# A fused attention kernel on one core: part 0's sums in its own steps, and the side jobs of each image in other steps

## The chip, the core and the metric

The kernel runs on one core of a Trainium2 chip. The metric is device time in microseconds (us) of that core, lower is better. The engines that matter are TensorE (PE: matmuls, with its weight loads PEld), VectorE (DVE), ScalarE (ACT), GpSimd (POOL), and the queue of SyncE (SP), which issues most transfers.

## The reference, cut to what matters

```python
def _L0_conv_ref(x, Wq, bq, Wk, bk, Wv, bv, gamma):      # x: (8, 128, 32, 32)
    xf = x.reshape(b, c, n)                              # n = 1024 pixels
    q = jnp.einsum('oc,bcn->bon', Wq, xf) + bq[None, :, None]      # 64 channels
    k = jnp.einsum('oc,bcn->bon', Wk, xf) + bk[None, :, None]
    v = jnp.einsum('oc,bcn->bon', Wv, xf) + bv[None, :, None]      # 128 channels
    attn = jax.nn.softmax(jnp.einsum('bci,bcj->bij', q, k), axis=-1)
    out = jnp.einsum('bcn,bmn->bcm', v, attn).reshape(b, c, h, w)
    return gamma * out + x
```

Eight images, each a self-attention over its 1024 pixels, all in fp32.

## The kernel before, in words

**Steps and parts.** Each image is cut into 16 steps (`STEPS`), 128 steps in all. A part is four steps (`PART_STEPS`) and 256 queries (`PART`): an image has four parts, and a step of a part takes two tiles of 128 keys. Two parts make a chunk of 512 queries. All five engines walk the same step numbers `s = 16*b + k` in a program written out by hand; semaphores tie them together. Nothing is scheduled by a planner: the order in the source is the order on each engine.

**Accuracy.** Values are split into a rounded high part and the rest. The scores of a step are two matmuls for each key tile (high and low halves of q and k stacked on the partitions, and the row of maxima as an extra row). ACT reads them twice (`exponentials`): once exact into `weight`, once rounded into `weight_hi`. The rest, `weight_lo`, is a subtraction (`low_weights`): on POOL for three steps of a part, and on DVE in the third (`low_on_dve`), where ACT writes the exact weights into a PSUM bank of the part's own sums instead (`exact_weights`, bank `sums[:, 1]` for even parts and `sums[:, 3]` for odd ones).

**PE's steps.** In step s PE makes the scores of step s+2 (`score_tile`, `AHEAD` = 2), one to three row maxima matmuls for later queries (`do_max`), the high sums of step s-2 (`sums_hi`, `LAG` = 2), at the end of a part the sixteen low sums (`sums_lo`), and the side jobs of the step: "qk" projects q and k of the image after next, half an image at a time; "v" projects V of the next image, by halves; "mt" turns maxima into a row (image 0 only; later images send them by DMA in `send_max_row`). In image 0 the maxima of images 0 and 1 have to be caught up with (`EARLY_MAXES`, 18 steps; an entry is chunk, first index, count).

**The two work banks.** Every maximum and every side job writes one of two PSUM banks, in turn (`WORK_ORDER`, `bank_of`). A job waits in `take_bank` until the job two places before it has been read out: a maximum by one DVE reduction (`maximum`); "qk" by ACT (`round_qk`) and then DVE (`rest_of_qk`); "v" by ACT (`round_v`) and then DVE (`rest_of_v`).

**The side chains.** ACT rounds x (`round_x`), POOL makes its rest (`rest_of_x`), PE projects, ACT and DVE round. Then SP spreads q and k over the partitions by DMA (`spread`; `spread_by_halves` for image 1, whose q and k and whose second half of image 0's V are projected straight into sums banks before and in steps 1 and 2). `round_qk` for the first half of an image waits until the spread of the image before has landed, since that spread reads the same tile. POOL makes the short copy of V (`short_values`) and adds the bias to x (`add_bias`). After a part's low sums ACT takes half of them (`take_low_sum`), DVE inverts and adds (`invert`, `add_low`), and `finish` writes y in the step `finish_step(part)`: six steps after the part's first, but eight for part 0. A sums bank is free when y of its part is done (`y_done`).

In step s, ACT does `exponentials(s + 2)`, then the rounding jobs; DVE the side jobs of step s-1, the maxima of s, `low_weights(s + 1)` if it is its turn, then `invert`, `add_low` and `finish`; POOL `low_weights(s + 1)` if it is its turn, then its side work.

Of the kernel before, what the change touches and what calls it, by code (L numbers as in the profile page):

```python
# [26 lines left out]
LAG = 2  # L27
# [21 lines left out]
               7: (2, 0, 2), 8: (2, 2, 2), 9: (2, 4, 1), 10: (2, 5, 1), 11: (2, 6, 2),  # L49
               12: (3, 0, 2), 13: (3, 2, 1), 14: (3, 3, 1), 15: (3, 4, 2), 16: (3, 6, 1), 17: (3, 7, 1)}  # L50

MAX_TURNS = {0: ("mt", 0, 1), 3: ("mt", 1, 0), 7: ("mt", 1, 1)}
# [11 lines left out]
def side_jobs(s):  # L64

    b, k = divmod(s, STEPS)
    jobs = []
    if s in MAX_TURNS:
        jobs.append(MAX_TURNS[s])
    if k in (6, 10) and b + 2 < BATCHES:  # L70
        jobs.append(("qk", b + 2, (6, 10).index(k)))
    if k in (11, 15) and b + 1 < BATCHES:
        jobs.append(("v", b + 1, (11, 15).index(k)))
    return jobs
# [17 lines left out]
def low_on_dve(s):  # L92
    return s % PART_STEPS == DVE_LOW
# [15 lines left out]
def finish_step(part):  # L109
    return PART_STEPS * part + PART_STEPS + AHEAD + (2 if part == 0 else 0)  # L110
# [29 lines left out]
def attention_program(nc, x, x_turned, Wq, bq, Wk, bk, Wv, bv, gamma, out):  # L140
# [9 lines left out]
    with ExitStack() as ctx:  # L150
# [275 lines left out]
        def _(pool):  # L426
# [67 lines left out]
            for s in range(ALL_STEPS):  # L494
# [5 lines left out]
                if k in (0, 12) and s > 0 and b + k // 12 < BATCHES:  # L500
                    short_values(b + k // 12, 1 - k // 12)
                if s in (4, 8):
                    add_bias((4, 8).index(s))
                if b == 0 and k in (5, 9) or b > 0 and k in (1, 5) and b + 2 < BATCHES:
                    rest_of_x(b + 2, (5, 9).index(k) if b == 0 else (1, 5).index(k))
                if b == 0 and k in (10, 13) or b > 0 and k in (9, 13) and b + 1 < BATCHES:
                    add_bias(2 * (b + 1) + k // 13)

        @block.tensor
        def _(pe):  # L510
# [87 lines left out]
            def sums_hi(s):  # L598
# [9 lines left out]
                if j == 0:  # L608

                    wait(pe, y_done, PAIR * (u - 1))  # L610
                    pe.wait_ge(weight_lo_done, low_count(s + DVE_LOW))
# [73 lines left out]
            pe.wait_ge(neg_max_done, CHUNK_TILES + 1)  # L685
            project_v(0, 1, sums[:, 0])
# [4 lines left out]
            for s in range(ALL_STEPS + LAG):  # L691
# [5 lines left out]
                if LAG <= s < ALL_STEPS:  # L697
                    if s == LAG:

                        pe.wait_ge(first_v_rest_done, 1)  # L700
                        pe.wait_ge(neg_max_done, CHUNK_TILES + PAIR)
                    if s == LAG + PART_STEPS:

                        pe.wait_ge(qk_lo_done, HALVES)
                    sums_hi(s - LAG)
                    if (s - LAG) % PART_STEPS == PART_STEPS - 1:
                        sums_lo(s - LAG)
                if s in (1, 2):
# [321 lines left out]
```

## Time and profile before

| | |
|---|---|
| time, median of 3 runs | 240.18 us (240.05 to 241.45) |
| time of the profiled execution | 239.82 us |
| its span in the profile | 238.0 us |
| PE busy | 221.8 us (93%) |
| ACT, POOL, DVE busy | 177.9, 177.5, 161.0 us (75%, 75%, 68%) |

The profiled execution's span covers all but 1.8 us of its own time. A busy time counts instructions of an engine; the matmuls of PE overlap in its pipeline, so that its pace is read from the starts of successive instructions rather than from their durations. All times of the trace are in us from the start of the span.

### The profile page before, as it was taken

Reading aid. Unit: us, or ns where it says so; the run is one execution under the profiler, and the core shown is the slowest. Engines: PE = TensorE matmul, PEld = TensorE weight load, DVE = VectorE, ACT = ScalarE, POOL = GpSimd, SP = SyncE. Lnnn points to the kernel's source line nnn. Section 1 sums busy time; section 2 is a strip of 40 time slices with the busy share of each in tenths; the row PEclk is TensorE's granted clock in tenths of the full one; section 3 lists DMA queues with packets and bytes.
Section 4 is the critical chain, followed back from the end, with each engine's and each line's share of the span. In section 5 each row is a group of like instructions: output and inputs, shape, how many; then the busy total and the mean of one; then the engine's idle time right before and its main releaser. Section 6 shows DMA issues by size and latency. Waiting matters only on the chain.

```text
span 238.0 us, 5352 instructions
## 1 busy us (share of the span) xinstructions
PE 221.8 (93%) x1864; PEld 205.0 (86%) x1864; DVE 161.0 (68%) x345; ACT 177.9 (75%) x342; POOL 177.5 (75%) x162
## 2 busy tenths in 40 slices
PE   6786958799999999999999999999999999999994
PEld 5464857599998999899998999899998999999994
DVE  1676556787776677777776677767776687676334
ACT  2486856668887798778877798778877788778980
POOL 8667665967877788778887787778886866886871
PEclk9999999999999999999999999999999999999999
DMA  3652640067700945048600964039400862100111
GB/s 95 212 211 64 156 136 1 4 144 166 223 0 3 234 120 178 2 106 208 214 10 0 218 153 164 2 89 221 139 0 0 196 159 88 49 0 3 44 48 44
DMA packets 17882, 24.43 MB, mean 103 GB/s; under 512 B 9920, under 2 KB 10688, under 8 KB 17856
## 3 DMA queue, kind: packets, MB, share of 16 engines
q1 hardware_dynamic: 17552, 23.96, 38.6%
q8 instruction: 15, 0.25, 0.5%
q10 hardware_dynamic: 304, 0.13, 0.2%
q14 instruction: 11, 0.09, 0.1%
HBM read 8.59 MB, written 4.19 MB: 54 GB/s over the span
## 4 chain that ended last, share of the span: by engine, by line
PE 80%; DVE 6%; ACT 4%; DMA 3%; issue 3%; POOL 2%; SPq 1%; ACTq 0%; POOLq 0%
PE sums L615 22%; PE sums L629 12%; PE scores L594 11%; PE scores L595 11%; PE work L550 10%; PE work L544 6%; ACT qk_hi L746 2%; DVE qk_lo L840 2%; DMA k_hione<-qk_hi 2%; DMA w_qk<-in_L_conv_Wk 1%; PE work L537 1%; PE work L539 1%; PE work L538 1%; PE sums L550 1%; DVE neg_max L849 1%
## 5 line engine op out<-in xcount | busy, mean ns | idle before, releaser
L476 POOL TENSOR_TENSOR weight_lo<-weight,weight_hi 128x512 bf16<-128x512 f32 x96 | 123.1, 1290 | 40.7 <-ACT weight_hi L788 40.6
L849 DVE TENSOR_REDUCE neg_max<-work 128x1 f32<-128x512 f32 x120 | 82.0, 686 | 12.2 <-PE work L550 12.2
L615 PEld LDWEIGHTS sums<-values,weight_hi 128*128 128x128 f32 x504 | 76.6, 189 | 6.7 <-issue 2.0
L615 PE MATMUL sums<-values,weight_hi 128*128 128x258 f32 x504 | 80.8, 282 | 1.7 <-DVE weight_lo L887 1.7
L788 ACT ACTIVATE weight_hi<-scores 128x512 fp32r<-128x512 f32 x128 | 76.4, 597 | 0.0
L594 PE MATMUL scores<-q_hihi,k_hilo 128*128 128x256 f32 x256 | 71.0, 300 | 0.5 <-ACT weight_hi L788 0.5
L595 PE MATMUL scores<-q_lomax,k_hione 128*128 128x256 f32 x256 | 66.2, 281 | 0.0
L785 ACT ACTIVATE weight<-scores 128x512 f32<-128x512 f32 x96 | 57.5, 599 | 10.0 <-PE scores L595 3.6
L550 PE MATMUL work<-k_hilo,q_hihi 128*128 128x512 f32 x120 | 48.4, 406 | 4.7 <-DVE qk_lo L840 3.3
L594 PEld LDWEIGHTS scores<-q_hihi,k_hilo 128*128 128x128 f32 x256 | 48.3, 189 | 2.1 <-issue 1.6
L595 PEld LDWEIGHTS scores<-q_lomax,k_hione 128*128 128x128 f32 x256 | 48.5, 189 | 1.0 <-issue 0.5
L629 PE MATMUL sums<-values_b,weight_lo 128*128 128x130 bf16 x496 | 34.4, 221 | 0.0
L629 PEld LDWEIGHTS sums<-values_b,weight_lo 128*128 128x128 bf16 x496 | 28.9, 98 | 1.4
L550 PEld LDWEIGHTS work<-k_hilo,q_hihi 128*128 128x128 f32 x120 | 22.6, 188 | 6.6 <-issue 2.7
L887 DVE TENSOR_TENSOR weight_lo<-sums,weight_hi 128x512 bf16<-128x512 f32 x32 | 22.0, 686 | 6.6 <-ACT weight_hi L788 6.6
L794 ACT ACTIVATE low_sum<-sums 128x256 f32<-128x256 f32 x31 | 11.9, 385 | 13.3 <-PE sums L629 13.3
L845 DVE TENSOR_TENSOR values<-work,values 128x512 fp32r<-128x512 f32 x14 | 9.7, 692 | 18.0 <-ACT values L757 18.0
L457 POOL TENSOR_TENSOR x_lo<-x_sb,x_hi 128x512 fp32r<-128x512 f32 x12 | 15.3, 1277 | 8.4 <-ACT x_hi L753 8.4
L785 ACT ACTIVATE sums<-scores 128x512 f32<-128x512 f32 x32 | 19.0, 592 | 3.0 <-DVE y_sb L912 2.3
L484 POOL TENSOR_TENSOR x_turned_sb<-x_turned_sb,gamma_bv 128x512 f32<-128x512 f32 x16 | 20.6, 1285 | 0.0
L912 DVE SCALAR_TENSOR_TENSOR y_sb<-sums,one_over,x_turned_sb 128x128 f32<-128x128 f32 x62 | 18.7, 343 | 0.7 <-DVE sums L892 0.4
L544 PE MATMUL work<-w_v_t,x_sb 128*128 128x128 f32 x112 | 15.4, 280 | 2.0 <-DVE qk_lo L840 1.9
(85 smaller groups left out, 162.4 us busy)
## 6 DMA issues: line engine op xcount, KB each, us to landing
x_turned_sb<-in_x_turned SPq DMA_DIRECT2D x8, 512.0 KB, 4.6
out<-y_sb SPq DMA_DIRECT2D x15, 256.0 KB, 3.4
x_sb<-in_x SPq DMA_DIRECT2D x7, 512.0 KB, 4.5
q_hihi<-qk_hi SPq DMA_DIRECT2D x12, 256.0 KB, 4.4
q_lomax<-qk_lo SPq DMA_DIRECT2D x7, 256.0 KB, 5.7
k_hione<-qk_hi SPq DMA_DIRECT2D x7, 256.0 KB, 5.2
k_hilo<-qk_hi SPq DMA_DIRECT2D x6, 256.0 KB, 3.2
k_hilo<-qk_lo SPq DMA_DIRECT2D x6, 256.0 KB, 5.1
```

The lines of the kernel that those rows point to most:

```text
L476: pool.tensor_tensor(weight_lo[:, r], weight[:, r], weight_hi[:, r], ALU.subtract).then_inc(weight_lo_pool_done, 1)
L484: pool.tensor_tensor(place, place, bias, ALU.add).then_inc(with_bias_done, 1)
L544: last = pe.matmul(place[:, tile(t)], image(n)[:, tile(half * CHUNK_TILES + t)], w_v_t[:, :], start=True, stop=True)
L550: pe.matmul(place, q_hihi[p][:, tile(t)], k_hilo[p][:, chunk(h)], start=True, stop=True).then_inc(mx_done, 1)
L594: pe.matmul(place, k_hilo[p][:, keys], q_hihi[p][:, queries], start=True, stop=False)
L595: last = pe.matmul(place, k_hione[p][:, keys], q_lomax[p][:, queries], start=False, stop=True)
L615: last = pe.matmul(sums[:, u % 2 * PAIR + it, 0:VCOLS], weight_hi[:, r, part_tile(kt, it)], values[p][:, key_tile(s, kt)], start=(j == 0 a ...
L629: last = pe.matmul(sums[:, u % 2 * PAIR + it, CHANNELS:VCOLS], weight_lo[:, i % RING, part_tile(kt, it)], values_b[p][:, key_tile(i, kt)], ...
L785: act.activation(exact_weights(s) if low_on_dve(s) else weight[:, r], scores[:, s % 2], ACT.Exp)
L788: act.activation(weight_hi[:, r], scores[:, s % 2], ACT.Exp).then_inc(weight_hi_done, 1)
L849: dve.reduce_max(neg_max[:, t, h:h + 1], place, AX.X, negate=True).then_inc(neg_max_done, 1)
L887: dve.tensor_tensor(weight_lo[:, r], exact_weights(s), weight_hi[:, r], ALU.subtract).then_inc(weight_lo_done, 1)
```

## The change: what it does

- Part 0 (steps 0 to 3): `sums_hi(s)` runs in step s itself and not in step s+2. All four low weights of this part are made on POOL (`low_on_dve` starts with part 1), so that its sums banks are not lent out, and `sums_hi` of part 0 no longer waits for them. The second half of image 0's V goes to bank `sums[:, 2]` (waiting for one more pair of first maxima), q and k of image 1 to banks 3 and 2. DVE takes the first maximum of chunk 1 ahead of the rest of V. The low sums of part 0 stay in step 5.
- y of part 0 is finished in step 6, not 8.
- Side jobs: q and k of the image after next in steps 7 and 11 (before 6 and 10), and in steps 10 and 13 of image 0; V of the next image in steps 3 and 15 (before 11 and 15), and in 7 and 15 of image 0. x is rounded in steps 4 and 8, and its rest made in 5 and 9, in every image (before, 0 and 4, 1 and 5 behind image 0). The short copies of V and the biases follow the new places.
- The early maxima are dealt out a little differently over steps 7 to 17, and two turns of maxima stand one step later (4 and 8).

```diff
--- before.py
+++ after.py
@@ -46,10 +46,13 @@
 
 EARLY = 18
 EARLY_MAXES = {0: (1, 1, 1), 1: (1, 2, 1), 2: (1, 3, 1), 3: (1, 4, 1), 4: (1, 5, 1), 5: (1, 6, 1), 6: (1, 7, 1),
-               7: (2, 0, 2), 8: (2, 2, 2), 9: (2, 4, 1), 10: (2, 5, 1), 11: (2, 6, 2),
-               12: (3, 0, 2), 13: (3, 2, 1), 14: (3, 3, 1), 15: (3, 4, 2), 16: (3, 6, 1), 17: (3, 7, 1)}
-
-MAX_TURNS = {0: ("mt", 0, 1), 3: ("mt", 1, 0), 7: ("mt", 1, 1)}
+               7: (2, 0, 1), 8: (2, 1, 2), 9: (2, 3, 2), 10: (2, 5, 1), 11: (2, 6, 2),
+               12: (3, 0, 1), 13: (3, 1, 1), 14: (3, 2, 2), 15: (3, 4, 1), 16: (3, 5, 2), 17: (3, 7, 1)}
+
+MAX_TURNS = {0: ("mt", 0, 1), 4: ("mt", 1, 0), 8: ("mt", 1, 1)}
+QK_STEPS, FIRST_QK_STEPS = (7, 11), (10, 13)
+V_STEPS, FIRST_V_STEPS = (3, 15), (7, 15)
+X_HI_STEPS, X_LO_STEPS = (4, 8), (5, 9)
 
 
 def max_jobs(s):
@@ -67,10 +70,11 @@
     jobs = []
     if s in MAX_TURNS:
         jobs.append(MAX_TURNS[s])
-    if k in (6, 10) and b + 2 < BATCHES:
-        jobs.append(("qk", b + 2, (6, 10).index(k)))
-    if k in (11, 15) and b + 1 < BATCHES:
-        jobs.append(("v", b + 1, (11, 15).index(k)))
+    qk_steps, v_steps = (FIRST_QK_STEPS, FIRST_V_STEPS) if b == 0 else (QK_STEPS, V_STEPS)
+    if k in qk_steps and b + 2 < BATCHES:
+        jobs.append(("qk", b + 2, qk_steps.index(k)))
+    if k in v_steps and b + 1 < BATCHES:
+        jobs.append(("v", b + 1, v_steps.index(k)))
     return jobs
 
 
@@ -90,7 +94,7 @@
 
 
 def low_on_dve(s):
-    return s % PART_STEPS == DVE_LOW
+    return s >= PART_STEPS and s % PART_STEPS == DVE_LOW
 
 
 def low_count(s):
@@ -107,7 +111,7 @@
 
 
 def finish_step(part):
-    return PART_STEPS * part + PART_STEPS + AHEAD + (2 if part == 0 else 0)
+    return PART_STEPS * part + PART_STEPS + AHEAD
 
 
 def max_count(chunk, i):
@@ -497,14 +501,18 @@
                     low_weights(s + 1)
                 if s == 0:
                     short_values(0, 1)
-                if k in (0, 12) and s > 0 and b + k // 12 < BATCHES:
-                    short_values(b + k // 12, 1 - k // 12)
-                if s in (4, 8):
-                    add_bias((4, 8).index(s))
-                if b == 0 and k in (5, 9) or b > 0 and k in (1, 5) and b + 2 < BATCHES:
-                    rest_of_x(b + 2, (5, 9).index(k) if b == 0 else (1, 5).index(k))
-                if b == 0 and k in (10, 13) or b > 0 and k in (9, 13) and b + 1 < BATCHES:
-                    add_bias(2 * (b + 1) + k // 13)
+                if k == 0 and b > 0:
+                    short_values(b, 1)
+                if k == (10 if b == 0 else 6) and b + 1 < BATCHES:
+                    short_values(b + 1, 0)
+                if s == 4:
+                    add_bias(0)
+                if k == (8 if b == 0 else 1):
+                    add_bias(HALVES * b + 1)
+                if k in X_LO_STEPS and b + 2 < BATCHES:
+                    rest_of_x(b + 2, X_LO_STEPS.index(k))
+                if k == 13 and b + 1 < BATCHES:
+                    add_bias(HALVES * (b + 1))
 
         @block.tensor
         def _(pe):
@@ -608,7 +616,8 @@
                 if j == 0:
 
                     wait(pe, y_done, PAIR * (u - 1))
-                    pe.wait_ge(weight_lo_done, low_count(s + DVE_LOW))
+                    if u > 0:
+                        pe.wait_ge(weight_lo_done, low_count(s + DVE_LOW))
                 pe.wait_ge(weight_hi_done, s + 1)
                 for kt in range(PAIR):
                     for it in range(PAIR):
@@ -682,8 +691,8 @@
             for s in range(AHEAD):
                 score_tile(s)
 
-            pe.wait_ge(neg_max_done, CHUNK_TILES + 1)
-            project_v(0, 1, sums[:, 0])
+            pe.wait_ge(neg_max_done, CHUNK_TILES + PAIR + 1)
+            project_v(0, 1, sums[:, PAIR])
             pe.wait_ge(first_hi_done, len(FIRST))
             for name, c, i in FIRST_MAXES:
                 do_max(c, i)
@@ -694,20 +703,24 @@
                 if s < ALL_STEPS:
                     for c, i in max_jobs(s):
                         do_max(c, i)
-                if LAG <= s < ALL_STEPS:
-                    if s == LAG:
-
-                        pe.wait_ge(first_v_rest_done, 1)
+                if s < PART_STEPS:
+                    if s == 0:
+
                         pe.wait_ge(neg_max_done, CHUNK_TILES + PAIR)
-                    if s == LAG + PART_STEPS:
+                    sums_hi(s)
+                elif PART_STEPS + LAG <= s < ALL_STEPS:
+                    if s == PART_STEPS + LAG:
 
                         pe.wait_ge(qk_lo_done, HALVES)
                     sums_hi(s - LAG)
-                    if (s - LAG) % PART_STEPS == PART_STEPS - 1:
-                        sums_lo(s - LAG)
-                if s in (1, 2):
-                    pe.wait_ge(neg_max_done, CHUNK_TILES + PAIR + s)
-                    project_qk(1, s - 1, sums[:, PAIR + s - 1])
+                if LAG <= s < ALL_STEPS and (s - LAG) % PART_STEPS == PART_STEPS - 1:
+                    sums_lo(s - LAG)
+                if s == 1:
+                    pe.wait_ge(neg_max_done, MAXES)
+                    project_qk(1, 0, sums[:, PAIR + 1])
+                if s == 2:
+                    pe.wait_ge(first_v_rest_done, 1)
+                    project_qk(1, 1, sums[:, PAIR])
                 if s < ALL_STEPS:
                     for job in side_jobs(s):
                         do_job(job)
@@ -778,8 +791,6 @@
                 if low_on_dve(s):
                     u = s // PART_STEPS
                     wait(act, y_done, PAIR * (u - 1))
-                    if u == 0:
-                        act.wait_ge(neg_max_done, CHUNK_TILES + PAIR)
                     if u == 1:
                         act.wait_ge(qk_lo_done, HALVES)
                 act.activation(exact_weights(s) if low_on_dve(s) else weight[:, r], scores[:, s % 2], ACT.Exp)
@@ -815,7 +826,7 @@
             write_max_rows(1, 0, 0, PART, scores[:, 1])
             exponentials(0)
             first_q(1, bank(0))
-            round_v(0, 1, sums[:, 0])
+            round_v(0, 1, sums[:, PAIR])
             exponentials(1)
 
             for s in range(ALL_STEPS):
@@ -823,13 +834,13 @@
                 if s + AHEAD < ALL_STEPS:
                     exponentials(s + AHEAD)
                 if s in (1, 2):
-                    round_qk(1, s - 1, sums[:, PAIR + s - 1])
+                    round_qk(1, s - 1, sums[:, PAIR + 2 - s])
                 if s >= LAG and (s - LAG) % PART_STEPS == PART_STEPS - 1:
                     take_low_sum((s - LAG) // PART_STEPS)
                 for job in side_jobs(s):
                     do_job(job)
-                if b == 0 and k in (4, 8) or b > 0 and k in (0, 4) and b + 2 < BATCHES:
-                    round_x(b + 2, (4, 8).index(k) if b == 0 else (0, 4).index(k))
+                if k in X_HI_STEPS and b + 2 < BATCHES:
+                    round_x(b + 2, X_HI_STEPS.index(k))
 
             store_last(act, 1)
 
@@ -952,11 +963,11 @@
             dve.wait_ge(first_hi_done, len(FIRST))
             dve.scalar_tensor_tensor(q_lomax[0][0:HEAD, chunk(1)], bank(0)[0:HEAD, :], b_qq[0:HEAD, :],
                                      q_hihi[0][0:HEAD, chunk(1)], ALU.add, ALU.subtract).then_inc(first_q_rest_done, 1)
-            dve.wait_ge(v_hi_done, HALVES)
-            dve.tensor_tensor(values[0][:, quarter(1), 0:CHANNELS], by_tiles(sums[:, 0]),
-                              values[0][:, quarter(1), CHANNELS:2 * CHANNELS], ALU.subtract).then_inc(first_v_rest_done, 1)
             for name, c, i in FIRST_MAXES:
                 do_max(c, i)
+            dve.wait_ge(v_hi_done, HALVES)
+            dve.tensor_tensor(values[0][:, quarter(1), 0:CHANNELS], by_tiles(sums[:, PAIR]),
+                              values[0][:, quarter(1), CHANNELS:2 * CHANNELS], ALU.subtract).then_inc(first_v_rest_done, 1)
 
             for s in range(ALL_STEPS):
                 b, k = divmod(s, STEPS)
@@ -966,7 +977,7 @@
                 for c, i in max_jobs(s):
                     do_max(c, i)
                 if s in (1, 2):
-                    rest_of_qk(1, s - 1, sums[:, PAIR + s - 1])
+                    rest_of_qk(1, s - 1, sums[:, PAIR + 2 - s])
                 if s + 1 < ALL_STEPS and low_on_dve(s + 1):
                     low_weights(s + 1)
                 if s >= LAG and (s - LAG) % PART_STEPS == PART_STEPS - 1:
```

## Rows read from the trace of the kernel before

**Rows 1.** The page: PE's busy time, and the chain that ended last by engine.

```profile
PE 221.8 (93%) x1864; PEld 205.0 (86%) x1864; DVE 161.0 (68%) x345; ACT 177.9 (75%) x342; POOL 177.5 (75%) x162
...
PE 80%; DVE 6%; ACT 4%; DMA 3%; issue 3%; POOL 2%; SPq 1%; ACTq 0%; POOLq 0%
```

**Rows 2.** Busy time over one image: length, then PE, PEld, DVE, ACT, POOL, clock.

```profile
71.80:98.80 27.00, 26.61 (x232) 25.15 (x232) 19.81 (x43) 21.91 (x42) 21.54 (x19) 1.00 0.46 118
```

**Rows 3.** Waits on PE: us in total, times, longest.

```profile
PE work L544 <- DVE qk_lo L840: 1.9, 5, 0.4
```

**Rows 4.** Timeline of PE, image 2: start, duration, instruction, idle before.

```profile
100.35 1.16 PE L544 MATMUL work<-w_v_t,x_sb 128*128 128x128 f32 x8 [0.39 <-DVE qk_lo L840]
...
102.53 0.28 PE L594 MATMUL scores<-q_hihi,k_hilo 128*128 128x256 f32 x1
...
103.00 0.42 PE L550 MATMUL work<-k_hilo,q_hihi 128*128 128x512 f32 x1
...
103.26 0.65 PE L615 MATMUL sums<-values,weight_hi 128*128 128x258 f32 x4
...
120.76 0.50 PE L550 MATMUL work<-k_hilo,q_hihi 128*128 128x512 f32 x1
```

**Rows 5.** The chain in order of time: start, us on the chain, what.

```profile
19.21 0.87 PE sums L533 x2
...
102.21 0.49 PE sums L615 x4
...
103.91 0.95 PE sums L629 x16
...
107.29 0.89 PE work L544 x8
```

**Rows 6.** Timeline of the start, steps up to the first part's end.

```profile
12.31 2.47 DVE L849 TENSOR_REDUCE neg_max<-sums 128x1 f32<-128x512 f32 x4
...
18.12 0.28 PE L555 MATMUL work<-identity_r,neg_max_r 128*1 128x128 f32 x2 [0.70 <-DVE neg_max L849]
...
20.83 0.75 DVE L840 SCALAR_TENSOR_TENSOR qk_lo<-sums,b_qk,qk_hi 128x512 fp32r<-128x512 f32 x1 [0.89 <-ACT qk_hi L746]
...
22.44 0.72 PE L615 MATMUL sums<-values,weight_hi 128*128 128x258 f32 x4 [1.66 <-DVE weight_lo L887]
...
29.09 0.37 PE L594 MATMUL scores<-q_hihi,k_hilo 128*128 128x256 f32 x1
```

**Rows 7.** Timeline of steps 7 to 18.

```profile
32.72 0.69 ACT L746 ACTIVATE qk_hi<-work,b_qk 128x512 fp32r<-128x512 f32 x1 [1.78 <-DMA k_hione<-qk_hi]
...
34.34 0.47 PE L550 MATMUL work<-k_hilo,q_hihi 128*128 128x512 f32 x1 [2.41 <-DVE qk_lo L840]
...
38.14 0.58 ACT L785 ACTIVATE sums<-scores 128x512 f32<-128x512 f32 x1 [2.33 <-DVE y_sb L912]
...
41.36 0.47 PE L537 MATMUL work<-x_hi,w_qk_hi 128*128 128x512 f32 x1 [0.46 <-POOL x_lo L457]
...
43.87 0.50 PE L550 MATMUL work<-k_hilo,q_hihi 128*128 128x512 f32 x1 [0.87 <-DVE qk_lo L840]
...
45.32 2.58 SPq L378 DMA_DIRECT2D q_lomax<-neg_max_r  x4
...
57.31 0.36 PE L594 MATMUL scores<-q_hihi,k_hilo 128*128 128x256 f32 x1
```

**Rows 8.** The page's groups: busy, mean ns of one, then idle before.

```profile
L476 POOL TENSOR_TENSOR weight_lo<-weight,weight_hi 128x512 bf16<-128x512 f32 x96 | 123.1, 1290 | 40.7 <-ACT weight_hi L788 40.6
```

**Rows 9.** Issue to landing of the maxima rows (L378), steps 11 to 19.

```profile
DMA to landing us min/median/max: 1.9/2.0/2.1
```

**Rows 10.** The spread and its reader one image on: SP and PE, timeline.

```profile
78.09 1.16 SPq L353 DMA_DIRECT2D k_hilo<-qk_lo  x1
...
84.85 0.40 PE L550 MATMUL work<-k_hilo,q_hihi 128*128 128x512 f32 x1
```

**Rows 11.** Issue to landing of the last spread that maxima need (L353).

```profile
DMA to landing us min/median/max: 4.9/5.1/6.3
```

## The prediction

> **What bounds the kernel now.** I read the busy times and the chain first, then PE's waits, then the start step by step. PE is busy for 93% of the span and the last chain lies on it for 80% [rows 1]. Behind the start an image takes 27.0 us, of which PE is busy for 26.6 and ACT, POOL and DVE for about 20 to 22 [rows 2]. So the bound is PE's stream of matmuls, none of which the change adds or removes: the time can move only by PE's stalls. Where they are: five times 0.4 us before a V job [rows 3], and many in the first 57 us, where step 18 starts at 57.31 [rows 7]. What a step costs PE when it never waits comes from one undisturbed step: scores 0.47 (102.53 to 103.00), a maximum 0.25 (103.00 to 103.26; 0.24 where nothing holds it) [rows 4], high sums 0.48, low sums 0.95, half a V 0.89, half of image 1's q and k 0.87 [rows 5]; half a q and k of a later image is three 512-column matmuls at the pace of the maximum, 0.7. ACT's two exponentials take about 0.6 each, from the one at 38.14 [rows 7]; with their overlap I use 1.2 a pair. Four DVE maxima take 2.47 [rows 6], so 0.62 one, 0.67 with a hand-off; a POOL subtraction 1.29 [rows 8].
>
> **Part 0's sums in its own steps.** Before, PE waits 0.70 for a work bank ahead of the first turn [rows 6] and 1.66 in step 2, where the high sums need the low weights of step 2, which DVE makes only behind `rest_of_qk` (20.83 to 21.58, itself idle for 0.89 behind ACT) [rows 6]. After, I walk the steps. The V half in bank 2 needs seven first maxima; four run from 12.31 to 14.78 [rows 6], so the seventh is read at about 14.2, before PE asks at 14.7: no cost. Step 0: scores from 16.5, maximum, high sums, done at 17.7; DVE has by then read the first maximum (0.67 sooner, as the rest of V now follows it), and the turn waits for nothing. Step 1: scores to 18.3, but the maximum's bank is read only behind the rest of V and one maximum, at 18.9: **a new stall of 0.6**. High sums and q and k end at 20.5. Step 2 ends at 22.6, step 3 (no side job) at 23.8. Step 4 has no sums; its turn waits for a maximum that DVE makes behind the second `rest_of_qk`, until 25.0 (0.5 of stall). Step 5 ends with the low sums at 26.9. Before, step 6 begins at 29.09 [rows 6]. **Gain so far 2.2.**
>
> The price of the move is one subtraction more on POOL. POOL makes low weights 0 to 3 by 22.1 in my walk and PE wants them at 25.9, so 1.29 is hidden with 3.8 to spare. It frees DVE by about a maximum's time before its second q and k. On the 1.29: POOL's subtractions average 1290 ns over 96 cases, beside a DVE that is busy two thirds of the time [rows 1, 8], so I see no stretching. The Trainium skill, "SBUF — State Buffer", section "SBUF: two separate sides", says the pair of ports that DVE and GpSimd share is an exclusive lock, taken on DVE's side by two-port modes or by two SBUF inputs. DVE's two-input instructions here have one input in PSUM, so by the rule as by the row nothing is added; if the lock did bite, each POOL subtraction could wait for a whole DVE instruction, 0.7 more, and the 3.8 us of cover would be eaten to about 1.
>
> **Steps 6 to 9: q and k of image 2 later, V of image 1 sooner.** Before, ACT's rounding of the q and k of step 6 waits until the spread of image 1 has landed (1.78 idle, start at 32.72), and PE waits 2.41 for the bank [rows 7]. After, q and k stand in step 10, which PE reaches at 35.5; the spread is issued about 1 us sooner than before and lands at about 31.7. That stall goes whole. What is late next: V in step 7 waits 0.4 for the maximum of step 6, which DVE makes behind `invert` and `add_low`; the maxima of step 8 wait for V's two roundings and one maximum, 0.8 in all. Step 10 starts at 35.5. Before, PE was through with step 9 at about 38.9: from 34.34 on the rest of step 7 is 0.8, step 8 with two maxima 1.45, step 9 with its low sums 2.15, and some 0.1 of refilling. **Gain 3.4 to 3.5** (2.2, plus 2.4, less 1.2, and V's 0.9 for q and k's 0.7 in these steps).
>
> **y of part 0 sooner.** Before, `exponentials(10)` writes into part 0's bank and waits 2.33 for y, until 38.14; PE then stalls for 0.5 before the scores of step 10 [rows 7]. After, y is done at 30.6 (low sum taken at 28.5, bias added on POOL at 27.3), while ACT asks at 31.5. That stall goes, and so does the 0.5 before 41.36 where the rest of x had waited behind that same ACT delay [rows 7]. **Gain 4.6 at the start of step 11** (37.5 against 42.1, which is 41.36 and q and k's 0.7).
>
> **Steps 11 to 18.** Removed: 0.9 at 43.87 behind q and k [rows 7] and about 0.9 behind V. New: the same kind behind the q and k of step 10 (0.9), one of 0.65 behind the V of step 15, and one of another kind: the row of image 1's maxima. Before, it is sent as soon as it is rounded, in four issues from 45.32 taking 2.58 [rows 7], and the last, issued 1.9 later, lands in 2.0 [rows 9], so 4.0 behind the rounding. The stretch in question (from the last maximum to the first scores of image 1) then holds a V and its wait more. After, the rounding is at 40.65, the row lands at 44.7, and PE, with fewer stalls between, asks at 43.9: **0.8 of new stall**. V and q and k change places at 0.1 to 0.2. Step 18 starts at about 52.65 against 57.31: still **4.65**. The spread of image 2 is now issued behind the q and k of step 13, from about 44.9; its last needed transfer is issued 1.9 later and lands in 4.9 to 6.3 [rows 11], so at 51.7 to 53.0. The maximum that reads it comes at 53.2. No cost, but with 0.2 to 1.5 to spare.
>
> **The later images.** Before, V directly follows q and k and waits for their bank: 0.39 of idle, and about 0.16 more (an estimate: the matmul ahead is still draining for 0.16, its 0.64 less the pace of 0.48) [rows 4], five times [rows 3]. After, it is a maximum two places behind the q and k of step 11, as it is already behind those of step 6: there it costs 0.2 (120.76, pushed back by 0.1, and its longer 0.50) [rows 4]. So 0.35 by five images is **1.75**. Between nothing (the hand-off only moves) and 2.75 (five holes of 0.55) the row of the same kind decides. V in step 3 stands in a part as V in step 15 does, which costs nothing. POOL's and ACT's moved jobs have the same lengths and POOL is idle for a fifth of an image [rows 2]. SP's order is unchanged: its spread waits for the scores of step 15 in any case, which by my count come 0.5 behind the rounding of the q and k of step 11.
>
> **The sum.** 4.65 + 1.75 = 6.4 off the profiled 239.82, so 233.4; the median was 0.36 above the profiled execution, so **233.8**. The start is between 2.2 (only its first term holds) and about 9 (none of my new stalls appears); I take 3.2 to 6.5 as its reasonable ends.
>
> **The rivals.**
> - **Hand-offs come back (0.22).** My walk finds seven small new stalls where DVE or ACT must read a bank; ACT with 1.2 of exponentials a step is barely slower than PE in the start. If each is 0.3 to 0.5 longer than I have, or the spread of image 2 is late, the start gives 2 to 3.5 and the images 1: 235.5 to 237. For it: the row of maxima and the spread both have under 1.5 to spare. Against: before, such waits of PE lie under 1 us each save two.
> - **More than the sum (0.10).** DVE gets ahead and the stalls in steps 1, 8 and 14 vanish: about 2.5 more, 231 to 232.
> - **Slower (0.05).** The spread of every image. Before, its last needed transfer (issued at 78.09 for the maximum at 84.85) has 0.5 to 1.9 to spare [rows 10, 11]. If q and k a step later (1.2 us, or 2.1 where a part ends) became what SP waits for, instead of the scores of step 15, PE would stand before the first maximum of images 2 to 7. It loses once the rounding is more than 0.5 behind those scores; beyond 1.1 a time for six images it eats the whole gain, 240 to 244. Against: my count has the rounding ahead of the scores.
> - **It does not do what it says (0.05).** If low weights or V still come last in part 0 and POOL is behind from step 4 on, the early gain is given back at the first y, and 238 to 240 stays.
> - My forecast, 232 to 235.5, has 0.58.
>
> The range 231.5 to 237.0 leaves out the slow ends and the fast tail of the second rival. A measurement of this kernel can tell about 1%, 2.4 us; within that are the cases above 237.8: same 0.07, slower by more 0.03, faster 0.90.
>
> **What would show it.** In the profile after: the high sums of step 0 near 17.2; step 6's scores near 26.9; ACT's first q and k of image 2 without a DMA wait; `exponentials(10)` without a wait for y; PE's first scores of image 1 at about 44.7, perhaps with a wait for the row; step 18 near 52.7; an image of 26.6 to 26.7 instead of 27.0, with no V job waiting for q and k. It would be wrong if image 1's maxima row or image 2's spread holds PE for more than 1 us, or if an image takes 27.0 or more.

## The result, and the profile after

The changed kernel takes 233.26 us (median of 4 runs, 232.98 to 233.76) against 240.12 us (median of 4): a ratio of 0.9707 with a 95% interval of 0.9666 to 0.9749. The prediction said 233.8, range 231.5 to 237.0. The profiled execution took 233.76 us, with a span of 232.0.

The page of the changed kernel, busy times and chain, which answer to [rows 1]:

```profile
PE 221.5 (96%) x1864; PEld 205.0 (88%) x1864; DVE 159.7 (69%) x344; ACT 178.1 (77%) x342; POOL 178.0 (77%) x163
...
PE 85%; DVE 6%; DMA 4%; ACT 2%; SPq 1%; issue 1%; ACTq 0%
```

PE's busy time is what it was, to 0.3 us, as it must be with the same 1864 matmuls; the span lost its stalls. DVE has one instruction less and POOL one more: the low weights of step 2.

Where the time went can be read by laying the two timelines of PE against each other at the start of each step (the first score matmul of the tile made in that step):

| step | before, us | after, us | difference |
|---|---|---|---|
| 0 | 16.48 | 16.72 | +0.24 |
| 6 | 29.09 | 26.86 | -2.23 |
| 10 | 39.48 | 35.11 | -4.37 |
| 11 | 42.14 | 37.08 | -5.06 |
| 14 | 50.07 | 44.70 | -5.37 |
| 18 | 57.31 | 52.80 | -4.51 |
| 34 | 84.29 | 79.31 | -4.98 |
| 66 | 138.32 | 132.41 | -5.91 |
| 98 | 192.34 | 185.51 | -6.83 |
| 117 | 220.17 | 213.35 | -6.82 |
| 118 | 222.06 | 215.98 | -6.08 |
| 125 | 229.87 | 223.80 | -6.07 |

Counted from step 0, the start gives 4.75 us by step 18. Then five images give 0.42 to 0.50 each, 2.32 in all. Then something takes 0.74 back in one step, 117 to 118. PE's waits in the changed kernel (us in total, times, longest):

```profile
PE work L558 <- DVE values L856: 1.4, 2, 0.7
PE scores L602 <- DMA q_lomax<-neg_max_r: 1.4, 2, 0.9
PE work L558 <- DVE qk_lo L851: 0.9, 1, 0.9
```

The start, as the timeline of the changed kernel shows it (start, duration, instruction, idle before and its releaser):

```profile
17.50 0.65 PE L624 MATMUL sums<-values,weight_hi 128*128 128x258 f32 x4
18.00 0.28 PE L563 MATMUL work<-identity_r,neg_max_r 128*1 128x128 f32 x2
18.96 0.50 PE L558 MATMUL work<-k_hilo,q_hihi 128*128 128x512 f32 x1 [0.15 <-DVE neg_max L860]
...
25.00 0.28 PE L563 MATMUL work<-identity_r,neg_max_r 128*1 128x128 f32 x2 [0.26 <-DVE neg_max L860]
...
25.94 1.11 PE L638 MATMUL sums<-values_b,weight_lo 128*128 128x130 bf16 x16
26.86 0.36 PE L602 MATMUL scores<-q_hihi,k_hilo 128*128 128x256 f32 x1
...
27.81 0.61 ACT L796 ACTIVATE weight<-scores 128x512 f32<-128x512 f32 x1
28.80 0.60 ACT L796 ACTIVATE weight<-scores 128x512 f32<-128x512 f32 x1
...
30.89 0.59 ACT L796 ACTIVATE sums<-scores 128x512 f32<-128x512 f32 x1
31.78 0.50 PE L558 MATMUL work<-k_hilo,q_hihi 128*128 128x512 f32 x1 [0.71 <-DVE values L856]
...
38.81 0.50 PE L558 MATMUL work<-k_hilo,q_hihi 128*128 128x512 f32 x1 [0.86 <-DVE qk_lo L851]
...
40.26 2.44 SPq L382 DMA_DIRECT2D q_lomax<-neg_max_r  x4
...
44.70 0.38 PE L602 MATMUL scores<-q_hihi,k_hilo 128*128 128x256 f32 x1 [0.85 <-DMA q_lomax<-neg_max_r]
...
49.89 0.50 PE L558 MATMUL work<-k_hilo,q_hihi 128*128 128x512 f32 x1 [0.71 <-DVE values L856]
...
52.80 0.36 PE L602 MATMUL scores<-q_hihi,k_hilo 128*128 128x256 f32 x1
```

The high sums of step 0 stand at 17.50, where the kernel before had its first at 22.44 [rows 6]. The turn follows without a wait. ACT's exponentials of step 10, which had idled 2.33 us for y [rows 7], start at 30.89 with no idle in front; ACT's first q and k of image 2 has no DMA wait either. What is left are three bank hand-offs of 0.7 to 0.9 us behind a V or a q and k, and a wait of 0.85 us for the row of maxima. A wait costs more than its listed idle, since idle is counted from the end of the last matmul in the pipeline and not from the time when the next could have started. The maximum at 37.56 takes 0.24 of PE's pace, so the next could start at 37.80; it starts at 38.81, a hole of 1.0 for 0.86 of idle. "With the refill" below means such a hole.

A later image in the changed kernel, by stretch from step 34 to step 50 (columns as in [rows 2]), and the V job and the maximum behind q and k that answer to [rows 4]:

```profile
79.31:105.91 26.60, 26.60 (x235) 25.21 (x232) 19.68 (x43) 21.92 (x42) 21.40 (x19) 1.00 0.46 120
```

```profile
97.50 0.50 PE L558 MATMUL work<-k_hilo,q_hihi 128*128 128x512 f32 x1
...
101.69 1.05 PE L552 MATMUL work<-w_v_t,x_sb 128*128 128x128 f32 x8
```

PE's busy time now fills the stretch: 26.60 of 26.60. The V job waits for nothing. The maximum of step 13 has a duration of 0.50 in place of 0.39: a small late start, without idle, is all that the q and k of step 11 cost.

### The profile page after: what moved, and what is told of

The parts are those of the page before. It is cut to its first block, busy times and chain, and to the rows that moved or that the text cites. A ratio compares the mean times of both kernels' runs of the same rounds, so it can differ in the third digit from the quotient of the medians.

```text
span 232.0 us, 5350 instructions
## 1 busy us (share of the span) xinstructions
PE 221.5 (96%) x1864; PEld 205.0 (88%) x1864; DVE 159.7 (69%) x344; ACT 178.1 (77%) x342; POOL 178.0 (77%) x163
## 4 chain that ended last, share of the span: by engine, by line
PE 85%; DVE 6%; DMA 4%; ACT 2%; SPq 1%; issue 1%; ACTq 0%
PE sums L624 24%; PE scores L602 12%; PE work L558 12%; PE sums L638 11%; PE scores L603 11%; PE work L552 5%; DMA q_lomax<-neg_max_r 3%; DVE neg_max L860 2%; SPq L382 1%; DMA w_qk<-in_L_conv_Wk 1%; PE work L546 1%; PE work L547 1%; PE work L545 1%; PE scores L656 1%; PE sums L558 1%; DVE values L856 1%
## 5 line engine op out<-in xcount | busy, mean ns | idle before, releaser
L796 ACT ACTIVATE weight<-scores 128x512 f32<-128x512 f32 x97 | 58.1, 599 | 11.4 <-PE scores L603 4.4
L558 PE MATMUL work<-k_hilo,q_hihi 128*128 128x512 f32 x120 | 49.0, 411 | 2.8 <-DVE values L856 1.4
L898 DVE TENSOR_TENSOR weight_lo<-sums,weight_hi 128x512 bf16<-128x512 f32 x31 | 21.3, 686 | 6.3 <-ACT weight_hi L799 6.3
L796 ACT ACTIVATE sums<-scores 128x512 f32<-128x512 f32 x31 | 18.4, 594 | 1.6 <-PE scores L603 1.4
L851 DVE SCALAR_TENSOR_TENSOR qk_lo<-work,b_qk,qk_hi 128x512 fp32r<-128x512 f32 x12 | 9.0, 750 | 13.2 <-ACT qk_hi L759 13.2
```

What stands on the lines that cost most here:

```text
L558: pe.matmul(place, q_hihi[p][:, tile(t)], k_hilo[p][:, chunk(h)], start=True, stop=True).then_inc(mx_done, 1)
L796: act.activation(exact_weights(s) if low_on_dve(s) else weight[:, r], scores[:, s % 2], ACT.Exp)
L898: dve.tensor_tensor(weight_lo[:, r], exact_weights(s), weight_hi[:, r], ALU.subtract).then_inc(weight_lo_done, 1)
```

## The experiments

Each ratio is against the kernel before on the same chip. In the series of the next four kernels the kernel before has a median of 241.15, because four of its seven executions have a mean granted clock of 0.984 to 0.993 (241.15 to 243.05 us) and the other three 1.0 (239.37 to 240.06). Those four ratios therefore flatter somewhat, and I read the sizes from the traces. "From step 0" below is the difference of two step starts, less their difference at step 0, so that the start of the profile (step 0 begins anywhere from 15.97 to 17.84 in these profiles) drops out.

### The later images by themselves, and the start by itself

`start_only` is the changed kernel with:

```diff
-QK_STEPS, FIRST_QK_STEPS = (7, 11), (10, 13)
-V_STEPS, FIRST_V_STEPS = (3, 15), (7, 15)
+QK_STEPS, FIRST_QK_STEPS = (6, 10), (10, 13)
+V_STEPS, FIRST_V_STEPS = (11, 15), (7, 15)
```

and x, the short copies and the biases of images 1 to 6 back in their old steps too.

> Images 1 to 6 have their side jobs back in the old steps (q and k in 6 and 10, V in 11 and 15, x in 0, 4 and 1, 5); image 0 and part 0 are as in the changed kernel. Theory of two separate gains: the start keeps its 4.5 us and the five holes of 0.46 us before V come back, 2.3 us in all, so 235.5. Rival, one gain: the later images run at 26.6 us because the start put the engines into another order, so they keep that pace and the time stays at 233.3.

Measured: 235.81 us, ratio 0.9806 (0.9743 to 0.9868). From step 0 it is 4.74 us ahead of before at step 18 and 4.7 ahead at step 98: nothing is won in the later images. Its waits and one image of it:

```profile
PE work L551 <- DVE qk_lo L851: 1.9, 5, 0.4
```

```profile
80.28:107.33 27.05, 26.66 (x234) 25.19 (x232) 19.82 (x43) 21.89 (x42) 21.48 (x19) 1.00 0.46 117
```

`later_only` is the kernel before with:

```diff
-    if k in (6, 10) and b + 2 < BATCHES:
-        jobs.append(("qk", b + 2, (6, 10).index(k)))
-    if k in (11, 15) and b + 1 < BATCHES:
-        jobs.append(("v", b + 1, (11, 15).index(k)))
+    qk_steps, v_steps = ((6, 10), (11, 15)) if b == 0 else ((7, 11), (3, 15))
+    if k in qk_steps and b + 2 < BATCHES:
+        jobs.append(("qk", b + 2, qk_steps.index(k)))
+    if k in v_steps and b + 1 < BATCHES:
+        jobs.append(("v", b + 1, v_steps.index(k)))
```

and x, the short copies and the biases of later images in the new steps.

> The kernel before, with only images 1 to 6 given the new steps for their side jobs. Two separate gains: 240.1 less 2.3 is 237.8, an image of 26.55 us, and no V job waiting for q and k. Rival, one gain: without the new start the hand-offs return and it stays at 240.

Measured: 237.23 us, ratio 0.9879 (0.9800 to 0.9958). Its image:

```profile
83.09:109.69 26.60, 26.60 (x234) 25.23 (x232) 19.70 (x43) 21.92 (x42) 21.44 (x19) 1.00 0.46 119
```

The five waits of V come with the old steps and go with the new ones, whatever the start is: 27.05 and 26.60. The start and the later images add (4.70 at step 98 in `start_only` and, from step 18 to step 98, 2.35 in `later_only`, beside 7.07 in the changed kernel), and the rival of one gain falls. The price is 0.45 in this image and 2.35 over the five, where I had 0.35 an image. `later_only` took 237.23 where 237.8 was expected; it gains 0.2 in step 7 already, ahead of these images.

### The two halves of the start

`old_jobs` is the changed kernel with image 0's side jobs as before:

```diff
-QK_STEPS, FIRST_QK_STEPS = (7, 11), (10, 13)
-V_STEPS, FIRST_V_STEPS = (3, 15), (7, 15)
+QK_STEPS, FIRST_QK_STEPS = (7, 11), (6, 10)
+V_STEPS, FIRST_V_STEPS = (3, 15), (11, 15)
```

and `EARLY_MAXES` and `MAX_TURNS` of the kernel before, the short copy of image 1's first V in step 12.

> The changed kernel, but image 0 has its early maxima, turns, q, k and V in the old steps; part 0's sums stay in their own steps. My theory: PE is 2.2 us sooner at step 6, but q and k of step 6 then wait for the spread of image 1, which lands only 1 us sooner, so 1.2 of the 2.2 is given back in step 7 (a wait of about 3.6 us where it was 2.4); with y sooner some 0.5 to 1 comes back: 236 to 236.7. Rival, the sums carry the start by themselves: 233.3 to 234.

Measured: 236.40 us, ratio 0.9832 (0.9766 to 0.9899).

```profile
31.46 0.69 ACT L759 ACTIVATE qk_hi<-work,b_qk 128x512 fp32r<-128x512 f32 x1 [2.43 <-DMA k_hione<-qk_hi]
33.08 0.47 PE L558 MATMUL work<-k_hilo,q_hihi 128*128 128x512 f32 x1 [2.69 <-DVE qk_lo L851]
```

The spread lands 1.26 us sooner than in [rows 7] (31.46 for 32.72), PE is there sooner still, and waits 2.69 in place of 2.41: from step 0, 2.4 us of gain at step 6 are 1.7 at step 8. My 3.6 was too much, the direction right. At step 18 it is 1.53 ahead.

But the wait is not all that this kernel pays. The same trace shows TensorE's granted clock fall from 2.4 to 1.2 GHz right behind it (first the two maxima and the four high sums of step 8, which take nearly twice as long as elsewhere; then the busy times of a stretch, columns as in [rows 2]):

```profile
34.95 1.05 PE L558 MATMUL work<-k_hilo,q_hihi 128*128 128x512 f32 x2
35.81 1.06 PE L624 MATMUL sums<-values,weight_hi 128*128 128x258 f32 x4
```

```profile
33.90:37.40 3.50, 3.50 (x18) 3.31 (x16) 1.67 (x3) 2.07 (x4) 2.24 (x3) 0.51 0.00 0
```

PE had stood idle for 2.69 us up to 33.08 and then worked for 0.9 us before the clock fell; it was back at about 37.4. Step 8 takes 2.68 us here and 1.50 in the kernel before, and step 9 some 0.3 more than its matmuls need, so about 1.5 us of the start's gain (an estimate from these step lengths) goes to the clock. All four executions of this kernel list a mean clock of 0.992 or 0.993. Without the slow stretch it would be about 3.0 ahead at step 18. I had not foreseen this, and the time inside the expected range is in part luck: the smaller wait and the clock make up for each other.

`old_part0` is the kernel before with all new side steps, part 0 unchanged (its sums two steps behind, low weights of step 2 on DVE, y in step 8):

```diff
-    qk_steps, v_steps = ((6, 10), (11, 15)) if b == 0 else ((7, 11), (3, 15))
+    qk_steps, v_steps = ((10, 13), (7, 15)) if b == 0 else ((7, 11), (3, 15))
```

on top of `later_only`, with `EARLY_MAXES` and `MAX_TURNS` of the changed kernel.

> The kernel before with all the new steps of the side jobs, image 0's too, but part 0 as before: sums two steps behind, its low weights of step 2 on DVE, y in step 8. My theory: the wait of 2.4 us in step 7 goes, smaller ones of up to 1.2 us come for it, and ACT's wait for y grows because the rest runs ahead of it: 235.8 to 237. Rival, the side jobs carry the start by themselves: 233.3 to 234.

Measured: 236.77 us, ratio 0.9848 (0.9771 to 0.9925).

```profile
22.72 0.72 PE L620 MATMUL sums<-values,weight_hi 128*128 128x258 f32 x4 [1.66 <-DVE weight_lo L892]
...
35.60 0.58 ACT L790 ACTIVATE sums<-scores 128x512 f32<-128x512 f32 x1 [2.64 <-DVE y_sb L917]
37.14 0.50 PE L555 MATMUL work<-k_hilo,q_hihi 128*128 128x512 f32 x1 [1.55 <-ACT q_lomax L767]
```

At step 18 it is 1.04 ahead. Step by step: from step 0 it gains 3.46 by step 8 (the wait for the spread is gone) and has lost 2.6 of it by step 10: 1.1 in step 8, where a maximum waits for the V of step 7 as in the changed kernel, and 1.5 in step 9, where ACT idles for y. So the halves do not add: 1.53 and 1.04 alone, 4.75 together. Of the 2.2 us between, about 1.5 is the slow clock of `old_jobs`; the other 0.7 or so is left to the waits. Each alone runs into a wait that the other takes away: `old_jobs` into that for the spread, `old_part0` into that for y. Part 0's half holds several things at once (sums in their own steps, low weights on POOL, y in step 6, other banks); only y and POOL's extra work are taken apart below.

### y of part 0

`late_y` is the changed kernel with:

```diff
-    return PART_STEPS * part + PART_STEPS + AHEAD
+    return PART_STEPS * part + PART_STEPS + AHEAD + (2 if part == 0 else 0)
```

> The changed kernel, with y of part 0 in step 8 again. My theory: DVE makes it at about 34, ACT's exponentials of step 10 ask at 31.5 and wait 2.5 us, PE loses 0.4 before the scores of step 10 and 0.3 to 0.6 more where ACT is late after that: 233.9 to 234.4. Rival, ACT has slack enough in this order: 233.3, no difference.

Measured: 235.09 us, ratio 0.9789 (0.9753 to 0.9824), in a series whose before was 239.81.

```profile
33.43 0.58 ACT L796 ACTIVATE sums<-scores 128x512 f32<-128x512 f32 x1 [2.64 <-DVE y_sb L923]
34.54 0.37 ACT L775 ACTIVATE q_lomax<-work 1x256 fp32r<-1x256 f32 x1
34.97 0.50 PE L558 MATMUL work<-k_hilo,q_hihi 128*128 128x512 f32 x1 [1.55 <-ACT q_lomax L775]
```

ACT's 2.6 us are as expected; their price for PE is not. From step 0 the kernel is 2.95 ahead at step 18 and not 4.75, so y in step 6 is worth 1.8 us in this order. The rows show the path I had overlooked: behind the exponentials on ACT is queued the row of a turn of maxima, and PE's second maximum of step 9 needs the bank that this row is read from. PE waits there, a step before the scores that I had watched. The kernel before did not have this path. Its turn stood in step 7, so ACT had read the row (35.44) before the exponentials that waited for y (38.14, [rows 7]), and PE's wait came only at the scores of step 10:

```profile
35.44 0.37 ACT L762 ACTIVATE q_lomax<-work 1x256 fp32r<-1x256 f32 x1 [1.06 <-PE work L555]
...
39.48 0.35 PE L594 MATMUL scores<-q_hihi,k_hilo 128*128 128x256 f32 x1 [0.45 <-ACT weight_hi L788]
```

The change moves that turn to step 8, behind the exponentials of step 10. Moving the turn without y, as `late_y` and `old_part0` do, makes the wait for y dearer.

### The waits that are left

Three places of PE's timeline invite an edit. `qk_11` is the changed kernel with the first of these edits, `max_15` with the second, `both` with the two:

```diff
-QK_STEPS, FIRST_QK_STEPS = (7, 11), (10, 13)
+QK_STEPS, FIRST_QK_STEPS = (7, 11), (11, 13)
```

```diff
-               12: (3, 0, 1), 13: (3, 1, 1), 14: (3, 2, 2), 15: (3, 4, 1), 16: (3, 5, 2), 17: (3, 7, 1)}
+               12: (3, 0, 1), 13: (3, 1, 1), 14: (3, 2, 2), 15: (3, 4, 2), 16: (3, 6, 1), 17: (3, 7, 1)}
```

> The changed kernel, with the first half of image 2's q and k in step 11 and not 10, behind the last two maxima of image 1's first chunk. My theory: those maxima no longer wait 0.86 us for the bank that q and k hold, the row of maxima leaves 1 us sooner, and PE's 0.85 us wait for it ahead of step 14's scores shrinks; of the two waits one to both go: 231.6 to 232.5. Rival, the wait for the bank moves to step 13 and the row is still late: 233.3.

> The changed kernel with two maxima in step 15 and one in step 16, as before the change. My theory: no maximum stands two places behind the V of step 15 in the same step, so the wait of 0.71 us (0.9 with the refill) in step 16 goes, and up to 0.2 comes back ahead of V: 232.4 to 232.7. Rival: V then waits for the reduction of step 15's first maximum as long as the maximum waited for V: 233.3.

> The two edits of the other kernels together: q and k in step 11, two maxima in step 15. If the waits are separate they add: 230.8 to 231.8. If a wait freed in steps 11 to 14 is only handed on to step 16 or to the spread of image 2: 232.2 or more.

Measured, in the series of `late_y`: 232.20 (ratio 0.9686, 0.9650 to 0.9723), 232.46 (0.9691, 0.9656 to 0.9727) and 232.19 (0.9668, 0.9629 to 0.9707). These intervals overlap, and `both` is no faster than `qk_11` by its median and 0.4 short of its forecast of 230.8 to 231.8; the times do not show that the edits add. The traces do: against the changed kernel, from step 0, the three are 0.59, 0.42 and 1.16 ahead at step 18, and the later steps keep that. In `qk_11` neither the bank of step 11 nor the row holds PE by more than 0.25 any longer, but this came up in their place:

```profile
44.69 0.50 PE L558 MATMUL work<-k_hilo,q_hihi 128*128 128x512 f32 x1 [0.86 <-DVE qk_lo L851]
```

It is the second maximum of step 14, two places behind the q and k of step 13. In the changed kernel that hand-off lay beside the wait for the row and cost nothing. So half of the rival came true: the wait moves, but the row is in time. In `max_15` V waits 0.34 for the maximum two places ahead of it, so 0.42 is left of the 0.9 that went.

`max_13` is `both` with the first of the next two edits, which takes that new wait away; `max_13_8` has the second too and thins out step 8:

```diff
-               12: (3, 0, 1), 13: (3, 1, 1), 14: (3, 2, 2), 15: (3, 4, 2), 16: (3, 6, 1), 17: (3, 7, 1)}
+               12: (3, 0, 1), 13: (3, 1, 2), 14: (3, 3, 1), 15: (3, 4, 2), 16: (3, 6, 1), 17: (3, 7, 1)}
```

```diff
-               7: (2, 0, 1), 8: (2, 1, 2), 9: (2, 3, 2), 10: (2, 5, 1), 11: (2, 6, 2),
+               7: (2, 0, 1), 8: (2, 1, 1), 9: (2, 2, 2), 10: (2, 4, 2), 11: (2, 6, 2),
```

> The kernel with q and k in step 11 and two maxima in step 15, and now two maxima in step 13 and one in step 14. In the pair of edits the second maximum of step 14 waited 0.9 us for the q and k of step 13, two places ahead of it. My theory: with one maximum in step 14 the same hand-off has a whole step, so 0.9 to 1.1 goes: 231.0 to 231.4. Rival: the spread of image 2 or the row of maxima is next in line, and holds PE as long: 232.1.

> As the last one, with the maxima of steps 7 to 11 dealt out as 1, 1, 2, 2, 2 and not 1, 2, 2, 1, 2, so that none stands two places behind the V of step 7 in step 8. My theory: the 0.71 us wait there becomes at most 0.3, because the turn of step 8 now takes the same bank 0.5 us later, and 0.3 to 0.6 goes: 230.5 to 231.0. Rival: DVE has two maxima in three steps running and the wait comes back in step 11: 231.2 or more.

> The changed kernel once more, as the yardstick of this series: 232.9 to 233.5. Its profile tells whether the wait of PE for the last row of maxima, near the scores made in step 118, is in every execution (then it is part of the change's price) or comes and goes with how long that transfer takes to land (0.7 us of scatter).

Measured: `max_13` 231.73 us (ratio 0.9662, 0.9644 to 0.9681), `max_13_8` 231.88 (0.9654, 0.9630 to 0.9678), the changed kernel again 232.77 (0.9719, 0.9693 to 0.9746). `max_13` beats the changed kernel with intervals that do not touch: 1.04 us by the medians, 1.35 at step 18 from step 0. That is 0.2 beyond `both` and not the 0.9 to 1.1 expected. The timeline of `max_13` in step 15 shows what came for it, on PE's weight loads:

```profile
46.22 0.19 PEld L558 LDWEIGHTS work<-k_hilo,q_hihi 128*128 128x128 f32 x1 [0.41 <-DVE neg_max L860]
...
47.34 0.97 PEld L552 LDWEIGHTS work<-w_v_t,x_sb 128*128 128x128 f32 x8 [0.34 <-DVE neg_max L860]
```

Both work banks are held by maxima that DVE has not reduced: it makes y of part 2 between them. So the next in line was neither of the rival's two, but DVE's queue. `max_13_8` is 0.55 us ahead of `max_13` at step 11 from step 0, and 0.20 at step 12; the times do not tell the two apart. Its 231.88 is where the rival had it (231.2 or more), and for the rival's reason: the wait comes back in step 11, where both the second maximum and q and k wait for reductions that DVE makes before and behind y of part 1.

```profile
37.85 0.19 PEld L558 LDWEIGHTS work<-k_hilo,q_hihi 128*128 128x128 f32 x1 [0.34 <-DVE neg_max L860]
...
38.96 0.19 PEld L545 LDWEIGHTS work<-x_hi,w_qk_hi 128*128 128x128 f32 x1 [0.35 <-DVE neg_max L860]
```

### POOL's cover

`twice_low` is the changed kernel with:

```diff
+        spare = sbuf("spare", [TILE, 2, CHUNK], bf16)
...
+                if s in (2, 3):
+                    pool.tensor_tensor(spare[:, s - 2], weight[:, r], weight_hi[:, r], ALU.subtract)
                 pool.tensor_tensor(weight_lo[:, r], weight[:, r], weight_hi[:, r], ALU.subtract).then_inc(weight_lo_pool_done, 1)
```

> The changed kernel, with POOL making the low weights of steps 2 and 3 twice, the first time into a spare tile: 2.6 us more on POOL, where my working says 3.8 us of cover lies between low weight 3 and the low sums that read it. My theory: no change, 232.9 to 233.5, and the high sums and the low sums of part 0 start when they did. Rival, POOL is already what the start waits for: 1 to 2.5 us slower.

Measured: 233.12 us (ratio 0.9720, 0.9702 to 0.9738), beside 0.9719 for the changed kernel in the same series.

```profile
20.00 1.27 POOL L482 TENSOR_TENSOR spare<-weight,weight_hi 128x512 bf16<-128x512 f32 x1
21.22 1.30 POOL L483 TENSOR_TENSOR weight_lo<-weight,weight_hi 128x512 bf16<-128x512 f32 x1
22.47 1.29 POOL L482 TENSOR_TENSOR spare<-weight,weight_hi 128x512 bf16<-128x512 f32 x1
23.71 3.78 POOL L483 TENSOR_TENSOR weight_lo<-weight,weight_hi 128x512 bf16<-128x512 f32 x3
```

Low weight 3 is ready at about 25.0 in place of 22.2, and PE's steps start where those of `changed_again` do, to 0.1 us, from step 0 to step 117. The fourth low weight of part 0 on POOL costs PE nothing, and each subtraction still takes 1.27 to 1.30 us.

### The wait near the end

The profile of the changed kernel, and that of its second series, at the scores made in step 118:

```profile
215.98 0.38 PE L602 MATMUL scores<-q_hihi,k_hilo 128*128 128x256 f32 x1 [0.55 <-DMA q_lomax<-neg_max_r]
```

```profile
214.98 0.36 PE L602 MATMUL scores<-q_hihi,k_hilo 128*128 128x256 f32 x1
```

The chain of the first shows the cause, an issue of 0.5 KB that takes 4.07 us to land where the usual is 2.0 [rows 9]:

```profile
211.22 0.60 SPq L382
211.82 0.04 issue
211.87 4.07 DMA q_lomax<-neg_max_r
215.94 0.04 issue
215.98 0.38 PE scores L602
```

In the second, step 118 follows with no idle, and from step 0 the kernel is 7.07 us ahead of before at step 119 and not 6.29. Of the other kernels' profiles, those of `old_jobs` and `qk_11` lose 0.7 to 0.8 there too; the other nine lose 0.1 or nothing. So this is scatter of the transfer, about 0.7 us where it strikes, and no part of the change's price. The profiled execution with it was also the slowest of its four (233.76). What makes that transfer late in some executions is open.

## Why the prediction was right

**PE as the bound, and time that moves only by its stalls.** Right: busy time 221.8 and 221.5.

**Part 0, gain 2.2 by step 6.** Measured 2.23, or 2.47 from step 0. The two stalls that I expected, 0.6 and 0.5, are there and smaller: the rows at 18.96 and 25.00 list 0.15 and 0.26 of idle, 0.3 and 0.4 with the refill. Low weight 3 was ready on POOL at 22.2 (walk: 22.1), the low sums began at 25.94 (walk: 25.9). The cover of 3.8 us was tested and held.

**Steps 6 to 9, gain 3.4 to 3.5.** Measured at step 10: 4.37 against a start of step 10 that y held up by 0.5, so 3.9, or 4.1 from step 0. (The items in my bracket add up to 3.2; the walk's own steps gave 3.4.) The wrong item is the wait of 0.4 ahead of V: there is none. The term behind it is ACT's pair of exponentials. I used 1.2 us, and two pairs in a row start 0.99 apart (27.81 and 28.80 in the changed kernel): durations of 0.6 overlap. So ACT, and with it the low sum, y and DVE's queue, ran up to 1 us ahead of my walk (the low sum was taken at 27.54, walk 28.5). That this is what spared V its wait follows from the order of the queues; no run tests it alone.

**y sooner, 1.1.** Right. The two waits that hung on y in the kernel before, listed with 0.45 and 0.46, are gone; with the refill they were 0.6 each, 1.2 to 1.3 in all, and the gain grows from 4.1 at step 10 (less the stall) to 5.3 at step 11. The 1.8 us that `late_y` costs is not this term but the price of a late y in the new order, where the turn of maxima stands behind the waiting exponentials. What failed is my expectation for `late_y`: I priced the wait by the one consumer I had watched, the scores of step 10, and not by everything queued behind ACT's instruction.

**Steps 11 to 18, no net gain.** The three new items are right: 0.86 for 0.9 behind q and k, 0.85 for 0.8 on the row of maxima (PE's first scores of image 1 at 44.70, walk 44.7), 0.71 for 0.65 behind V. The spread of image 2 cost nothing. The balance is not right. From step 0 the gain is 5.30 at step 11 and 4.75 at step 18, so this stretch gives back 0.55. My own items say as much: 0.9 and 0.9 removed, 0.9, 0.65 and 0.8 new, 0.1 to 0.2 for V against q and k, which is a loss of about 0.4; yet I carried 4.6 on as 4.65. At step 11 the walk was 0.7 too cautious (4.6 for 5.30). The two slips cancel, and that step 18 came at 52.80 for 52.65 is in part luck.

**The later images, 1.75.** Measured 2.32. The term that was mis-sized is the 0.2 for a maximum behind the q and k of step 11: it costs about 0.1, since 0.46 is left of the hole of 0.55.

**The sum.** 4.75 and 2.32 are 7.1 where I had 6.4; the median moved by 6.9. Of the rivals, the returning hand-offs held in `old_jobs` and `old_part0`, where half of the change is missing, and not in the whole. The spread of every image stayed covered: no wait of PE for it is listed.

## What to carry to other kernels

When one engine is the bound and never changes its work, write its steps down by hand with the pace of a calm stretch, and carry the other engines' queues along. The waits placed that way were each within 0.4 us here; check the walk against the trace at several steps and not only at its end, where slips can cancel. Two edits that free the same stretch of a start can be worth more together (4.75 here) than the sum of the two apart (1.53 and 1.04), because each alone can run into a wait that the other takes away, so price them as a pair and test them as a pair. Before you put such a difference down to waits, look at the granted clock of each trace: of the 2.2 us missing here about 1.5 was the clock. Price a wait by everything queued behind the waiting instruction, and deal the jobs over two alternating banks so that nothing in the same step stands two places behind a job with two readers.

## What the runs showed of the hardware

**A long wait can cost the clock as well.** In the trace of `old_jobs` the granted clock fell to 1.2 GHz for about 3.4 us after PE had idled 2.69 us and worked 0.9 us; in that of the kernel before, with 2.41 us of idle at the same place [rows 7], it stayed at 2.4 GHz. Over the three series of experiments 8 of 28 executions of the kernel before list a mean clock of 0.983 to 0.993 and take 240.55 to 243.37 us, where the other 20 take 239.16 to 240.40. All nine of the changed kernel list 1.0, and so does every execution of the kernels without a wait of 2 us on PE in step 7, to within 0.003; `later_only`, which keeps that wait, has one of four at 0.993 (239.18 us). So the change probably also spares such executions 1 to 3.5 us. That is argued from the mean clocks: no trace of the kernel before with a fallen clock was kept.

**A small transfer's landing scatters.** The landing of a 0.5 KB transfer inside the chip, 1.9 to 2.1 us in [rows 9], reaches 2.5 to 4.1 us at its longest in these fourteen profiles, 3.9 in the kernel before itself; a schedule with under 1 us to spare behind it, as ahead of step 118, shows that as scatter of 0.7 us from one execution to the next. The start of the first step also moves, from 15.97 to 17.84 us into the span: two profiles are comparable to 0.1 us only once that is taken off.
